# Attention with the values stationary and the probabilities moving: result by channel, sums from a block of ones

## What is computed

```
win = x by windows                                   # (8*16 windows, 64 tokens, 128 channels)
q, k, v = split(layernorm(win) @ in_w.T + in_b)      # 8 heads of 16 channels
attn = softmax(q @ k.T / 4)                          # per window and head, 64 x 64
o = attn @ v
y = win + o @ out_w.T + out_b
y = y + silu(layernorm(y) @ fc1_w.T + fc1_b) @ fc2_w.T + fc2_b     # hidden size 256
```

## Time and profile before

| | |
|---|---|
| median of 3 runs | 367.18 us |
| profiled execution | 368.02 us |
| its span (first to last instruction) | 366.2 us |
| mean granted clock of PE | 0.984 |
| busy: PE, PEld, DVE, ACT, POOL | 346.6, 297.5, 284.5, 245.8, 166.8 us |
| one image in the steady part | 41.7 us |

### The profile page before, as it was taken

How to read it: one execution, slowest core, us unless ns; L and a number is a source line. 1 busy time by engine, 2 the same in 40 slices (tenths; PEclk the granted TensorE clock), 3 DMA queues, 4 the chain that set the end, 5 groups by cost and what they waited for, 6 DMA issues and landing times. The chain is left out here.

```text
span 366.2 us, 9776 instructions
## 1 busy us (share of the span) xinstructions
PE 346.6 (95%) x3352; PEld 297.5 (81%) x3352; DVE 284.5 (78%) x850; ACT 245.8 (67%) x449; POOL 166.8 (46%) x177
## 2 busy tenths in 40 slices
PE   4698999999999999999999999999999999999884
PEld 3588888888888888878888888988888888888663
DVE  5666779888788888888788887888788987877562
ACT  5557567684968659594877759594777759583470
POOL 6506084636445442646444543644444444542430
PEclk9998799999999999999999999999999999999997
DMA  4224030312223031212214032221214031110011
GB/s 133 64 67 111 1 88 32 79 40 54 62 79 93 7 99 66 64 50 52 63 66 106 0 86 86 57 58 42 73 57 105 9 83 61 46 45 2 0 60 57
DMA packets 31858, 21.98 MB, mean 60 GB/s; under 512 B 22432, under 2 KB 23776, under 8 KB 31840
## 3 DMA queue, kind: packets, MB, share of 16 engines
q1 hardware_dynamic: 31840, 21.75, 21.7%
HBM read 4.95 MB, written 4.19 MB: 25 GB/s over the span
## 5 line engine op out<-in xcount | busy, mean ns | idle before, releaser
L685 PE MATMUL p_score<-kd_h,qd_h 128*128 128x128 f32 (+1 forms) x512 | 57.0, 255 | 1.3 <-DMA qd_h<-q_h 1.3
L512 POOL TENSOR_TENSOR hid_l<-hid,hid_h 128x512 fp32r<-128x512 f32 x30 | 40.4, 1368 | 37.2 <-ACT hid_h L1099 35.3
L685 PEld LDWEIGHTS p_score<-kd_h,qd_h 128*128 128x128 f32 (+1 forms) x512 | 51.1, 167 | 6.4 <-issue 1.4
L1305 DVE TENSOR_REDUCE row_max<-p_score 128x8 f32<-128x512 f32 x64 | 44.0, 687 | 15.6 <-PE p_score L685 15.6
L1065 ACT ACTIVATE probs<-p_scoreT 128x512 f32<-128x512 f32 x64 | 38.6, 603 | 23.5 <-PE p_scoreT L708 23.3
L723 PEld LDWEIGHTS p_attn<-vd,probs 128*64 128x64 f32 x1024 | 36.6, 141 | 16.3 <-issue 9.6
L723 PE MATMUL p_attn<-vd,probs 128*64 128x34 f32 x1024 | 45.7, 245 | 1.8 <-ACT probs L1065 1.4
L517 POOL TENSOR_TENSOR y_l<-y,y_h 128x512 fp32r<-128x512 f32 x15 | 19.2, 1283 | 60.1 <-ACT y_h L1079 60.1
L504 POOL TENSOR_SCALAR kd_l<-k_l,head_a 128x512 fp32r<-128x512 f32 x15 | 23.6, 1573 | 38.5 <-DVE k_l L1287 24.1
L704 PE MATMUL p_scoreT<-qd_h,kd_h 128*128 128x256 f32 x128 | 39.9, 312 | 0.0
L496 POOL TENSOR_TENSOR rstd<-rstd,minus_half 128x4 f32<-128x4 f32 (+1 forms) x33 | 35.5, 1075 | 2.8
(11 more groups left out here) (260 smaller groups left out, 905.9 us busy)
## 6 DMA issues: line engine op xcount, KB each, us to landing
qd_h<-q_h SPq DMA_DIRECT2D x64, 64.0 KB, 2.0
qd_l<-q_l SPq DMA_DIRECT2D x64, 64.0 KB, 2.0
vd<-v_tok SPq DMA_DIRECT2D x64, 64.0 KB, 2.2
out<-out_sb SPq DMA_DIRECT2D x15, 256.0 KB, 2.1
x_in<-in_x SPq DMA_DIRECT2D x14, 256.0 KB, 2.8
x_first<-in_x SPq DMA_DIRECT2D x2, 256.0 KB, 2.8
fc_rows<-in_L_conv_fc_w SPq DMA_DIRECT2D x2, 128.0 KB, 2.7
out<-out_sb SPq DMA_DIRECT2D x2, 128.0 KB, 2.1
```

Source lines behind the costliest of these rows:

```text
L512: pool.tensor_tensor(hid_l[:, t], hid[:, t], hid_h[:, t].bitcast(F32), ALU.subtract).then_inc(hid_low[t], 1)
L685: last = pe.matmul(p_score[0:rows, 2 * KEYS * j:2 * KEYS * (j + 1)], qd_h[:, h.par, j, 2 * KEYS * p:2 * KEYS * p + rows], kd_h[:, h.par, 2 ...
L1305: dve.tensor_reduce(row_max[:, p % 2], p_score[:].rearrange("row (h k) -> row h k", h=HEADS), AXIS_X, ALU.max).then_inc(max_ready[p], 1)
```

## The change

1. `b_attn` swaps its operands. `vd` (32 columns: two heads of 16 channels) is stationary and `probs` (64 columns: the queries of one window) moves. The result has channels on partitions, four groups of 32 partitions for the four head pairs, and the windows side by side.
2. The column of ones in `vd` goes (`VB` = 16). Four more matmuls have a block of ones, `sum_block`, stationary and both windows' `probs` (128 columns) moving, so that every channel's row gets the sum of its head. They stand first in the block.
3. `b_norm` takes the reciprocal of 128 x 128 sums instead of 128 x 8 and multiplies 128 x 128, without a broadcast. It writes `o`, by channel, in SBUF.
4. `c_transpose` is gone, with its semaphore `oT_ready`. `c_o` on ACT and DVE read `o` in SBUF instead of a PSUM bank, and wait for `b_norm`. The waits for the bank that `c_transpose` had move to `c_project`.
5. In the start-up POOL sets two small blocks of ones instead of four strips in `vd`, and SP waits for one memset before the first `spread_v`.

```diff
-VB = DH + 1
+VB = DH
...
-        inv_sum = sb("inv_sum", [128, HEADS])
-        o_tok = sb("o_tok", [128, PAIRS, C])
+        sum_block = sb("sum_block", [128, 2, DH])
+        inv_sum = sb("inv_sum", [C, 2 * KEYS])
+        o = sb("o", [C, HALF])
...
-                sp.wait_ge(v_const_set, 5)
+                sp.wait_ge(v_const_set, 1)
...
                 pe.wait_ge(probs_ready[p], h.n())
                 if p == 0:
+                    if h.follows(1):
+                        pe.wait_ge(o_ready[PAIRS - 1], h.n(1))
+                    else:
+                        pe.wait_ge(sum_set, 3)
+                else:
+                    pe.wait_ge(o_ready[p - 1], h.n())
+                for j in range(QUADS):
+                    pe.matmul(p_attn[32 * j:32 * j + 32, 2 * KEYS:4 * KEYS], sum_block[:].rearrange("row a d -> row (a d)"),
+                              probs[:, p % 2, :, j, :], start=True, stop=True)
+                if p == 0:
                     pe.wait_ge(v_dma, h.n(times=16 * 4))
-                    if h.follows(1):
-                        pe.wait_ge(o_tok_ready[PAIRS - 1], h.n(1))
-                else:
-                    pe.wait_ge(o_tok_ready[p - 1], h.n())
-                for j in range(QUADS):
-                    for win in range(2):
-                        last = pe.matmul(p_attn[64 * win:64 * win + 64, 2 * VB * j:2 * VB * (j + 1)],
-                                         probs[:, p % 2, win, j, :],
+                for win in range(2):
+                    for j in range(QUADS):
+                        last = pe.matmul(p_attn[32 * j:32 * j + 32, KEYS * win:KEYS * (win + 1)],
                                          vd[:, h.par, 2 * p + win, :, :, j].rearrange("row a d -> row (a d)"),
-                                         start=True, stop=True)
+                                         probs[:, p % 2, win, j, :], start=True, stop=True)
                 last.then_inc(attn_ready[p], 1)
...
-            def c_transpose(h):
-                pe.wait_ge(o_tok_ready[h.tiles[-1]], h.loop.half(h.c).n())
-                if h.early:
...
-                for t in h.tiles:
-                    last = pe.transpose(c_banks(h)[0][:, C * t:C * t + C], o_tok[:, t, :], ident[:])
-                last.then_inc(oT_ready, 1)
...
             def c_o(h):
-                act.wait_ge(oT_ready, h.n())
+                act.wait_ge(o_ready[h.tiles[-1]], h.loop.half(h.c).n())
...
-                act.activation(o_h[:, h.cols], c_banks(h)[0][:, h.cols], ACT.Copy).then_inc(o_high, 1)
+                act.activation(o_h[:, h.cols], o[:, h.cols], ACT.Copy).then_inc(o_high, 1)
...
-                heads = p_attn[:, 0:HEADS * VB].rearrange("row (h d) -> row h d", h=HEADS)
-                dve.reciprocal(inv_sum[:], heads[:, :, DH]).then_inc(inv_ready[p], 1)
+                dve.reciprocal(inv_sum[:], p_attn[:, 2 * KEYS:4 * KEYS]).then_inc(inv_ready[p], 1)
                 dve.wait_ge(inv_ready[p], h.n())
-                dve.tensor_tensor(o_tok[:, p, :].rearrange("row (h d) -> row h d", h=HEADS), heads[:, :, 0:DH],
-                                  inv_sum[:].unsqueeze(2).to_broadcast([128, HEADS, DH]), ALU.mult
-                                  ).then_inc(o_tok_ready[p], 1)
+                dve.tensor_tensor(o[:, 2 * KEYS * p:2 * KEYS * (p + 1)], p_attn[:, 0:2 * KEYS], inv_sum[:], ALU.mult
+                                  ).then_inc(o_ready[p], 1)
...
-                dve.tensor_tensor(o_l[:, h.cols], c_banks(h)[0][:, h.cols], o_h[:, h.cols].bitcast(F32), ALU.subtract
+                dve.tensor_tensor(o_l[:, h.cols], o[:, h.cols], o_h[:, h.cols].bitcast(F32), ALU.subtract
```

More of the change, by code:

```diff
@@ L241, in build @@
         ident_set, const_ready = sem("ident_set"), sem("const_ready")
-        q_zero_set, v_const_set = sems("q_zero_set", 2), sem("v_const_set")
+        q_zero_set, v_const_set, sum_set = sems("q_zero_set", 2), sem("v_const_set"), sem("sum_set")
         wT_ready, wT_kept, bias_ready, bias_kept = sem("wT_ready"), sem("wT_kept"), sem("bias_ready"), sem("bias_kept")
@@ L256, in build @@
         scoreT_ready, probs_ready = sems("scoreT_ready", 4), sems("probs_ready", 4)
-        attn_ready, inv_ready, o_tok_ready = sems("attn_ready", 4), sems("inv_ready", 4), sems("o_tok_ready", 4)
-        oT_ready, o_high, o_low, proj_ready, y1_ready = (
-            sem("oT_ready"), sem("o_high"), sem("o_low"), sem("proj_ready"), sem("y1_ready"))
+        attn_ready, inv_ready, o_ready = sems("attn_ready", 4), sems("inv_ready", 4), sems("o_ready", 4)
+        o_high, o_low, proj_ready, y1_ready = sem("o_high"), sem("o_low"), sem("proj_ready"), sem("y1_ready")
         yT_ready, ln2_stats, ln2_mv, ln2_var, ln2_rstd, yn_tok_set = (
@@ L464, in _, with set_sum_blocks @@
             pool.memset(vd[:], 0.0).then_inc(v_const_set, 1)
-            pool.wait_ge(v_const_set, 1)
-            def set_sum_columns(s):
+            pool.memset(sum_block[:], 0.0).then_inc(sum_set, 1)
+            pool.wait_ge(sum_set, 1)
+            def set_sum_blocks():
                 for a in range(2):
-                    pool.memset(vd[64 * a:64 * a + 64, s, :, a, DH, :], 1.0).then_inc(v_const_set, 1)
+                    pool.memset(sum_block[64 * a:64 * a + 64, a, :], 1.0).then_inc(sum_set, 1)
             def waited():
@@ L537, in prologue @@
                 pool.wait_ge(w_ready, 1)
-                set_sum_columns(0)
-                set_sum_columns(1)
-                pool.wait_ge(v_const_set, 5)
+                set_sum_blocks()
+                pool.wait_ge(sum_set, 3)
                 rstd1_of(loop.half(1))
@@ L715, in b_attn, with c_project @@
                 if p == 0:
-                    pe.wait_ge(v_dma, h.n(times=16 * 4))
-                    if h.follows(1):
-                        pe.wait_ge(o_tok_ready[PAIRS - 1], h.n(1))
-                else:
-                    pe.wait_ge(o_tok_ready[p - 1], h.n())
-                for j in range(QUADS):
-                    for win in range(2):
-                        last = pe.matmul(p_attn[64 * win:64 * win + 64, 2 * VB * j:2 * VB * (j + 1)],
-                                         probs[:, p % 2, win, j, :],
+                    if h.follows(1):
[8 more added lines that the diff above has]
+                if p == 0:
+                    pe.wait_ge(v_dma, h.n(times=16 * 4))
+                for win in range(2):
+                    for j in range(QUADS):
+                        last = pe.matmul(p_attn[32 * j:32 * j + 32, KEYS * win:KEYS * (win + 1)],
                                          vd[:, h.par, 2 * p + win, :, :, j].rearrange("row a d -> row (a d)"),
-                                         start=True, stop=True)
+                                         probs[:, p % 2, win, j, :], start=True, stop=True)
                 last.then_inc(attn_ready[p], 1)
-            def c_transpose(h):
-                pe.wait_ge(o_tok_ready[h.tiles[-1]], h.loop.half(h.c).n())
+            def c_project(h):
+                pe.wait_ge(o_high, h.n())
+                pe.wait_ge(o_low, h.n())
+                pe.wait_ge(w_ready, 2)
                 if h.early:
@@ L935, in epilogue @@
                 c_fc1(c, 1)
-                c_transpose(early)
                 b_attn(b, 3)
                 d_kvT(loop, -1)
-                c_transpose(late)
                 d_bT(loop, -1)
@@ L1322, in b_norm @@
                     if h.follows(1):
-                        dve.wait_ge(oT_ready, h.n(1))
-                heads = p_attn[:, 0:HEADS * VB].rearrange("row (h d) -> row h d", h=HEADS)
-                dve.reciprocal(inv_sum[:], heads[:, :, DH]).then_inc(inv_ready[p], 1)
+                        dve.wait_ge(o_high, h.n(1))
+                dve.reciprocal(inv_sum[:], p_attn[:, 2 * KEYS:4 * KEYS]).then_inc(inv_ready[p], 1)
                 dve.wait_ge(inv_ready[p], h.n())
-                dve.tensor_tensor(o_tok[:, p, :].rearrange("row (h d) -> row h d", h=HEADS), heads[:, :, 0:DH],
-                                  inv_sum[:].unsqueeze(2).to_broadcast([128, HEADS, DH]), ALU.mult
-                                  ).then_inc(o_tok_ready[p], 1)
+                dve.tensor_tensor(o[:, 2 * KEYS * p:2 * KEYS * (p + 1)], p_attn[:, 0:2 * KEYS], inv_sum[:], ALU.mult
+                                  ).then_inc(o_ready[p], 1)
             def c_o(h):
```

3 lines of the change are left out of this document (removed).

## The result

The changed kernel takes 389.18 us (median of 4 runs, 385.82 to 390.97), the kernel before beside it 367.24 (365.93 to 368.01): a ratio of 1.0585, 95% interval 1.055 to 1.062. The forecast was 384, its own range 377 to 390. The profiled execution took 389.06 with a span of 387.3; the span before was 366.2, so 21.1 us are to be explained. The mean granted clock of PE fell from 0.984 to 0.967; the run of 385.82 had 0.980.

The account below looks back on a forecast made before the run. PE was taken as the bound between hand-overs, whose chain is last b_attn, b_norm(3), row maximum, b_score(1). 2.2 an image times 7 (15.5) plus 1.1 for the closing half on 368.0 gave 384.6, forecast 384, range 377 to 390.

Parts of the forecast that it names:

- The 2.2 an image: Added time per image: even half 1.46 plus odd half 0.75, times 7 overlapping images.
- Transposes worth nothing: Removing 6.8 us of PE transposes (L739) gains nothing, since PE then waits for the row maximum instead.
- The reciprocal: In b_norm on DVE, widened from 128x8 to 128x128: 0.96 us each, +0.77 a time, 64 times.
- B: Rival: cheap reciprocal, +0.13 a time; 367 us, up to 376 with o_l held behind POOL; chance 0.15.
- Even half, 1.54: b_norm(1), through yn_l, and b_norm(3) each add 0.77, so the row maximum and b_score(1) come 1.54 us later.
- Odd half, 0.45: b_norm(3)'s 0.77 less the idle 0.32 before the row maximum: hand-over +0.45 us.
- maximum 0: DVE's row maximum of b_score(0), 0.68 us at 200.82, for which PE's b_score(1) waits at the hand-over.
- `o_l` behind POOL, 0.5 in one hand-over: Odd-to-even hand-over: o_l, both inputs in SBUF, is held until POOL finishes at 183.65; c_project starts some 0.5 later.
- The block, -0.08: b_attn on PE: 24 passes four abreast, last start at 0.385 against 0.465 us, -0.08 a block.
- C: Rival: b_attn's column groups run only two abreast, 0.44 more a block than taken; 397 us, chance 0.17.
- a gain of 0.20: PE in an odd half: 4 x 0.08 from the b_attn blocks less 0.12 for another column arrangement.
- D, the clock: Rival: the clock falls in PE's new waits before b_score(1), 3.3 an image, 23 more; 407 us, chance 0.07.

Follow-up runs that it names:

- copy_ol_from_psum: Changed kernel with a copy instead of the 128x128 reciprocal and o_l reading its bank in PSUM; 368.0 us, ratio 0.999 to 1.003.
- reciprocal_pair1_only: The kernel of copy_ol_from_psum with the real reciprocal in b_norm(1) alone; 373.5 us, ratio 1.010 to 1.020.
- after_norm1_before_k: Changed kernel with b_norm(1) moved ahead of k_l (and of bT in odd halves) on VectorE; 389.2 us, ratio 1.048 to 1.062.
- before_ol_from_sbuf: Kernel before, transposes kept, with o_l subtracting o_h from o_tok in SBUF instead of from the PSUM bank; 379.1 us, ratio 1.028 to 1.032.
- block_same_group_next: The kernel of copy_ol_from_psum with both windows of a head pair one behind the other in b_attn's value passes; 371.6 us, ratio 1.007 to 1.017.
- reciprocal_pair3_only: The kernel of copy_ol_from_psum with the real reciprocal in b_norm(3) alone; 386.6 us, ratio 1.047 to 1.056.

## Why the prediction was right, and where its steps were not

- **Forecast.** 15.5 + 1.1 = 16.6 was forecast and 21.1 measured: 2.2 an image too, 13.2 in six, 2.4 for two falls, and 5.4 in the rest, of which a third fall some 1.2. Without these falls the sum would have been 17.4. So 3.6 of the missing 4.5 us are falls, which puts the median near the upper end of the range.
- **The 2.2 an image.** The chains at the hand-overs are the right ones, but that their sum came out to the tenth is luck. Two terms were too large, the even half's by 0.46 and the even-to-odd hand-over's by 0.05. Four were too small by 0.55 together: 0.16 in the odd half's hand-over, 0.16 for what POOL holds, and 0.20 and 0.03 for gains of PE that came out smaller. The bullets below take them one by one.
- **Transposes worth nothing.** Right. copy_ol_from_psum shows it to within the 0.08 of its copy: 368.0.
- **The reciprocal.** 0.944 us against 0.96, right, and B is out. The Trainium skill ("VectorE: DVE Perf Modes", First, the fixed hardware budget), with its iterated divide, had pointed to this reading; the trace agrees.
- **Even half, 1.54.** Too much. The hand-over is 0.72 later, as the 0.77 said. The other 0.77, by way of `yn_l` and fc1, was 0.31 (reciprocal_pair1_only: 0.27). The step that failed is that the whole 0.77 reaches `yn_l`: the widening behind `b_norm(1)` took 0.81 in the kernel before, where it began 0.16 behind the start of POOL's `kd_l`, and takes 0.42 at 204.39, where it begins 0.82 behind it, and so gives half of it back. In the kernel before:

```profile
194.71 1.57 POOL L504 TENSOR_SCALAR kd_l<-k_l,head_a 128x512 fp32r<-128x512 f32 x1 [1.92 <-DVE k_l L1287]
194.87 0.81 DVE L1316 CAST max_wide<-row_max 128x512 bf16<-128x512 f32 x1
```

  And PE didn't wait before fc1 but at `b_attn(2)`, for the single bank `p_attn`; I had not asked who waits for `b_norm(1)` itself. The wait before fc1 that was forecast stands right behind it, and shows in after_norm1_before_k.
- **Odd half, 0.45.** Too little: 0.61 in the hand-over. I counted the idle 0.32 before maximum 0 as room, but 0.27 us of idle stay there.
- **`o_l` behind POOL, 0.5 in one hand-over.** The rule and the place were right, the size and the form not. Alone it costs 0.81 and 0.64 (before_ol_from_sbuf), 11.2 us; with the reciprocal it turns into a held widening at 0.33 in both hand-overs. That I took only one of them came out near by chance: 2 x 0.33 against 0.5.
- **The block, -0.08.** First to last start was forecast at 0.385; it is 208.14 + 0.42 - 0.22 (a pass) - 207.90 = 0.44, against 0.465. So 0.03 was gained a block and not 0.08. Four abreast holds, C is out. In an odd half 0.07 is gained up to the last block and 0.07 lost behind it, where a gain of 0.20 was forecast. That the two passes of one matmul don't hold each other was read from two starts within 20 ns, but the rows don't say which matmul these two belong to; that is open, and block_same_group_next shows that closeness on a group has a price.
- **D, the clock.** I gave 0.07 to a fall in each image, 407. Nothing like that, but three falls in eight images, and five in reciprocal_pair3_only. It should have been a term of the sum with its own bounds, not only a rival: the earlier trace rows had shown a fall behind 4.00 us with 2.86 busy, and the new hand-over has 2.72 of 4.00. Why one such stretch is followed by a fall and the next isn't stays open.

Of the signs that were named, a longer `o_l` and an idle PE before fc1 did not come; the reciprocal, DVE's busy time (334 against 330), the starts in fours and the wait for `row_max` did.

No version here is faster than the kernel before. copy_ol_from_psum says how little there is to win: with a 275 ns copy for the reciprocal it ties. An operation of the old 193 ns was not tried. My estimate of what it would give is 1.6 us at most, from the 0.23 by which the image of that run is longer than before.

## To carry to other kernels

A removal pays only if the engine it frees isn't waiting there already, and the cheap way to test it is the change with its costs taken away, not the change itself. When a result is laid out anew, count the elements that each slow operation now touches (8 to 128 here), and for every operand that moves from PSUM to SBUF look at what GpSimd does at that moment. Costs measured one at a time (18.9 and 11.2) may overlap (21.9) where one delays the other past the same neighbour.

## What was not expected of the hardware

- The reciprocal's price per element is steady over the whole range: (944 - 193) / 120 = 6.3 ns and (995 - 944) / 8 = 6.4 ns.
- A held DVE instruction isn't tied to its form: `o_l` (two SBUF inputs) and the widening (float32 to bfloat16, SBUF to SBUF) both wait for `hid_l` (1.47 instead of 0.69 us, 1.33 instead of 0.43), and in these runs the first one that starts early in a `hid_l` takes the wait. Started 0.82 into POOL's `kd_l`, the widening took 0.42, as it does alone; that edge wasn't tried.
- Two hand-overs with equal busy time and equal idle time on PE differ in whether the clock falls afterwards (2.72 and 2.74 above).
- Filling an idle stretch of PE with useless transposes gave 5 us, 1.1 of them by a shorter image and the rest with the falls (389.2 to 384.1).
